# Attention projections for two batches at once, with buffers, banks and weight replacement dealt over pairs of slots

## What is computed

```
q, k, v = x @ Wq.T, x @ Wk.T, x @ Wv.T          # 16 heads: 128 plain + 64 rotary features, v 128
q_rope, k_rope = rotate(q_rope), rotate(k_rope)  # y1 = x1*c - x2*s, y2 = x1*s + x2*c
scores = q_nope @ k_nope / sqrt(128) + q_rope @ k_rope / sqrt(64)
out = softmax(scores) @ v
x   = x + out @ Wo.T
```

## Time and profile before

| | us |
|---|---|
| Time, median of 3 runs | 671.25 (671.13 to 673.66) |
| Profiled execution | 672.77 |
| Its span in the trace | 671.0 |
| PE busy | 657.5 (98%) |
| PEld busy | 633.7 (94%) |
| DVE busy | 439.2 (65%) |
| ACT busy | 410.7 (61%) |
| POOL busy | 246.4 (37%) |

### The profile page before, as it was taken

How to read it: one execution, slowest core, us unless ns; L and a number is a source line. 1 busy time by engine, 2 the same in 40 slices (tenths; PEclk the granted TensorE clock), 3 DMA queues, 4 the chain that set the end, 5 groups by cost and what they waited for, 6 DMA issues and landing times. The chain is left out here.

```text
span 671.0 us, 15275 instructions
## 1 busy us (share of the span) xinstructions
PE 657.5 (98%) x5297; PEld 633.7 (94%) x5297; DVE 439.2 (65%) x968; ACT 410.7 (61%) x1085; POOL 246.4 (37%) x279
## 2 busy tenths in 40 slices
PE   8999999999999999999999999999999999999995
PEld 8989999999999999999999899999997799999995
DVE  5665557557666656765666576556559986556877
ACT  4566677666775666866667864333689964333553
POOL 2741862134363033533328554212361462222011
PEclk9999999999999999999999999999999999999998
DMA  7074665336444435634354404100156200000000
GB/s 254 28 201 160 209 172 149 110 107 184 148 138 122 133 98 176 180 112 139 95 166 146 111 1 151 32 0 0 40 192 254 79 1 1 1 1 0 1 33 31
DMA packets 38173, 69.74 MB, mean 104 GB/s; under 512 B 3441, under 2 KB 22641, under 8 KB 37873
## 3 DMA queue, kind: packets, MB, share of 16 engines
q1 hardware_dynamic: 37696, 68.38, 33.4%
q10 hardware_dynamic: 432, 0.79, 0.4%
HBM read 52.18 MB, written 16.97 MB: 103 GB/s over the span
## 5 line engine op out<-in xcount | busy, mean ns | idle before, releaser
L312 PE MATMUL PJ<-xTh,WBh 128*128 128x256 f32 x364 | 106.7, 293 | 0.0
L314 PE MATMUL PJ<-xTh,WBl 128*128 128x256 f32 x364 | 103.0, 283 | 0.0
L313 PE MATMUL PJ<-xTl,WBh 128*128 128x256 f32 x364 | 102.8, 282 | 0.0
L830 POOL TENSOR_TENSOR stage<-stage 128x256 f32<-128x256 f32 x32 | 24.5, 765 | 165.6 <-DVE stage L697 165.6
L590 ACT ACTIVATE probs<-probs,rinv 128x256 f32<-128x256 f32 x128 | 58.4, 508 | 26.7 <-DVE rinv L713 26.7
L1208 PE MATMUL UG<-xTh,WBh 128*128 (+1 forms) x256 | 73.6, 288 | 0.3 <-PEq L54 0.3
L1211 PE MATMUL UG<-xTh,WBl 128*128 (+1 forms) x256 | 72.4, 283 | 0.0
L1209 PE MATMUL UG<-xTl,WBh 128*128 (+1 forms) x256 | 72.4, 283 | 0.0
L1280 ACT ACTIVATE ga<-UG 128x256 f32<-128x256 f32 x64 | 24.5, 383 | 75.1 <-PE UG L1211 75.1
L312 PEld LDWEIGHTS PJ<-xTh,WBh 128*128 128x128 f32 x364 | 69.6, 191 | 0.6 <-issue 0.2
L313 PEld LDWEIGHTS PJ<-xTl,WBh 128*128 128x128 f32 x364 | 69.6, 191 | 0.0
(11 more groups left out here) (320 smaller groups left out, 2389.5 us busy)
## 6 DMA issues: line engine op xcount, KB each, us to landing
K<-scr_k SPq DMA_DIRECT2D x60, 256.0 KB, 4.4
raw<-in_w_att SPq DMA_DIRECT2D x37, 256.0 KB, 4.7
Q<-scr_q SPq DMA_DIRECT2D x15, 512.0 KB, 7.6
stage<-scr_m SPq DMA_DIRECT2D x6, 768.0 KB, 4.1
scr_q<-rot_h SPq DMA_DIRECT2D x30, 128.0 KB
scr_q<-rot_l SPq DMA_DIRECT2D x30, 128.0 KB
scr_k<-rot_h SPq DMA_DIRECT2D x30, 128.0 KB
scr_k<-rot_l SPq DMA_DIRECT2D x30, 128.0 KB
```

The source lines that it names most:

```text
L312: pe.matmul(out, ah, bh, start=(i == 0), stop=False)
L313: pe.matmul(out, ah, bl, start=False, stop=False)
L314: last = pe.matmul(out, al, bh, start=False, stop=(i == n - 1))
L830: pool.tensor_tensor(y[:, 0:S], c[:, 0:S], sn[:, S:2 * S], ALU.subtract).then_inc(rope_sum, 1)
```

## The change

Queries, keys and rotary parts are projected for a pair of batches at once: one product streams 512 columns (two batches of 256 tokens) against one weight tile, where before two products streamed 256 each. The pair holds for slots 2 to 15. For that:

- slots come in pairs, an **even** slot k and the **odd** slot behind it. In an even slot TensorE projects four pieces of queries and keys in steps 0 and 1, and in steps 2 and 3 the rotary parts of the next pair in four halves (`rope_half`). In an odd slot it projects eight pieces, two in each step: two of values of its own batch, four of queries and keys, two of values. The output projection moves to step 2 (`OUT_STEP`), the addition to the residual to step 3 (`ACC_STEP`).
- the two halves of a rotary part lie in two neighbouring banks, 512 columns each: part 0 (queries) in PJ0 and PJ1, part 1 (keys) in PJ1 and PJ2. VectorE takes from such a pair of banks first one batch, then the other (`rope_part`), with two multiplications for each as before.
- `QKh[:, 0]` and `QKl[:, 0]` hold heads 0 and 1 of both batches, `[:, 1]` heads 2 and 3, where before the index was the parity of the slot.
- the rotary work of a pair is spread over both its slots on ScalarE and GpSimd; `rot_h` and `rot_l` are used twice for each pair. SyncE spills 12 times 128 KB before the first fill of a pair, and 4 times behind it.
- weights are replaced over the slots with k % 4 of 1, 2 and 3, one or two at a time, and their loads are issued over four slots.

```diff
+        def pieces(k, j):
+            if k == 15 or k % 2 == 0 and j > (2 if k == 14 else 1):
+                return []
+            return [2 * j, 2 * j + 1]
+        def has_rope(k):
+            return k % 2 == 0 and k < 14
...
-                if k < 14:
-                    spill(s + 2, k + 2, 0)
-                    spill(s + 2, k + 2, 1)
+                if has_rope(k):
+                    t, n = s + 2, 2 * (s + 2)
+                    spill(t, k + 2, 0, n, 0)
+                    spill(t + 1, k + 3, 0, n + 1, 1)
+                    spill(t, k + 2, 1, n + 2, 0)
+                    fill(t, k + 2)
+                    spill(t + 1, k + 3, 1, n + 3, 1)
+                elif k < 14:
                     fill(s + 2, k + 2)
...
+            def project_two(out, at, col, b):
+                w, toks = slice(col * P, (col + 1) * P), slice(b * S, (b + 2) * S)
+                return three(out[:, :], [(WBh[:, at + t, w], WBl[:, at + t, w]) for t in range(KT)],
+                             [(xTh[:, t, toks], xTl[:, t, toks]) for t in range(KT)])
+            def rope_half(s, k, p, half):
+                b = (k + 2) % 4
+                if p == 0 and half:
+                    if k == 0:
+                        pe.wait_ge(x_split, B)
                     if b == 0:
+                        pe.wait_ge(w_split, GP * group_of(s + 2) + 2)
+                    pe.wait_ge(part_split, 6 * s + 8)
+                elif p == 0:
+                    pe.wait_ge(part_split, 6 * s + 10)
+                elif not half:
+                    pe.wait_ge(rope_prod, 2 * s + 6)
+                last = project_two(PJ[ROPE_BANK[p] + half], 0, 2 * p + half, b)
+                if not half:
+                    last.then_inc(rope_ready, 1)
...
@@ TensorE's emit
                     scores(s, k, j)
+                    if has_rope(k) and j >= 2:
+                        rope_half(s, k, j - 2, 1)
+                    for i in pieces(k, j)[:1]:
+                        piece(s, k, i)
                     if k > 0 or j >= 1:
                         turn_probs(u - 1, (j - 1) % 4, first=(k == 0 and j == 1))
+                    if has_rope(k) and j >= 2:
+                        rope_half(s, k, j - 2, 0)
+                    for i in pieces(k, j)[1:]:
+                        piece(s, k, i)
+                    if j == OUT_STEP and k > 0:
                         output(s - 1, k - 1, first=(k == 1))
...
@@ ScalarE's part
+            def rope_part(t, k, i):
+                act.wait_ge(rope_sum, 2 * (2 * t + i) + 2)
+                rot_free(act, t, k, i)
...
@@ VectorE's emit
+                    if k % 2 and k < 14 and j == 0:
+                        rope_part(s + 1, 3)
...
                     if j in EARLY_MAX:
                         row_max(u + 1, j + 1)
-                    if j == ROPE_STEP and k < 14:
-                        part(s + 2, k + 2, 1)
+                    if has_rope(k) and j >= 2:
+                        rope_part(s + 2, 2 * (j - 2))
+                    for i in pieces(k, j)[1:]:
+                        part(s, k, i)
                     if (k > 0 or j >= 2) and not (k == 14 and j == 1):
                         oT(u - 2, k if j >= 2 else k - 1, (j - 2) % 4)
+                    if has_rope(k) and j == 2:
+                        rope_part(s + 2, 1)
```

More of the change, by code:

```diff
@@ L119, in attention @@
         rope_lo = sem("rope_lo")
-        spill_q = sem("spill_q")
-        spill_k = sem("spill_k")
+        spill_done = [sem(f"spill_done{i}") for i in range(2)]
         stack_q = [sem(f"stack_q{i}") for i in range(2)]
@@ L208, in _, with spill @@
         def _(sp):
-            def spill(s, k, i):
-                scr, spilled = ((scr_q, spill_q), (scr_k, spill_k))[i]
-                for part, src, done in ((0, rot_h, rope_hi), (1, rot_l, rope_lo)):
-                    sp.wait_ge(done, 2 * s + i + 1)
+            def spill(s, k, i, m, at):
+                scr = (scr_q, scr_k)[i]
+                for part, src, ready in ((0, rot_h, rope_hi), (1, rot_l, rope_lo)):
+                    sp.wait_ge(ready, m + 1)
                     for half in range(2):
-                        sp.dma_start(scr[k % 2, 2 * part + half].rearrange("p j n -> j p n"),
-                                     src[:, i, half, :].bitcast(F32)).then_inc(spilled, 16)
+                        sp.dma_start(scr[k % 4, 2 * part + half].rearrange("p j n -> j p n"),
+                                     src[:, at, half, :].bitcast(F32)).then_inc(spill_done[k % 2], 16)
             def fill(s, k):
@@ L359, in piece @@
-            def piece(s, k, p):
-                b = k % 4
-                out = bank_of(k, p)
-                bank_free(s, k, p)
-                if b == 0 and p % 2 == 0:
-                    pe.wait_ge(w_split, GP * (s // 4 if isinstance(s, int) else group[0]) + 2 + p)
-                if p < 6:
-                    last = project(out, p, slice(b * S, b * S + S))
-                else:
-                    rows = slice(b * S + (p - 6) * P, b * S + (p - 5) * P)
-                    last = three(out[:, :], [(xTh[:, t, rows], xTl[:, t, rows]) for t in range(KT)],
-                                 [(WBh[:, 6 + t, :], WBl[:, 6 + t, :]) for t in range(KT)])
+                    pe.wait_ge(x_split, slot + 1)
@@ new lines, in first_rope, with first_piece @@
+                    if slot == 0:
+                        pe.wait_ge(w_split, 2)
+                if slot:
+                    pe.wait_ge(rope_prod, p + 1)
+                project(first_rope_bank(p), p, slice(slot * S, slot * S + S)).then_inc(rope_ready, 1)
+            def first_piece(p):
+                if p == 6:
+                    pe.wait_ge(part_split, 1)
+                if p == 7:
+                    pe.wait_ge(part_split, 2)
+                if p % 2 == 0:
+                    pe.wait_ge(w_split, 2 + p)
+                if p < 6:
+                    last = project(first_bank(p), p, slice(0, S))
+                else:
+                    last = values_in(first_bank(p), p - 6)
+                last.then_inc(piece_ready, 1)
@@ new lines, in values_in @@
+            def values_in(out, tile):
+                rows = slice(tile * P, (tile + 1) * P)
+                return three(out[:, :], [(xTh[:, t, rows], xTl[:, t, rows]) for t in range(KT)],
+                             [(WBh[:, 6 + t, :], WBl[:, 6 + t, :]) for t in range(KT)])
+            def project_two(out, at, col, b):
+                w, toks = slice(col * P, (col + 1) * P), slice(b * S, (b + 2) * S)
+                return three(out[:, :], [(WBh[:, at + t, w], WBl[:, at + t, w]) for t in range(KT)],
+                             [(xTh[:, t, toks], xTl[:, t, toks]) for t in range(KT)])
@@ L373, in piece, with query, key @@
                 last.then_inc(piece_ready, 1)
+            def query(part, k, j, rows):
+                if k < 2:
+                    return part[:, k, j, rows]
+                return part[:, j // 2, 2 * (j % 2), (k % 2) * S + rows.start:(k % 2) * S + rows.stop]
+            def key(part, k, j):
+                if k < 2:
+                    return part[:, k, j, S:2 * S]
+                return part[:, j // 2, 2 * (j % 2) + 1, (k % 2) * S:(k % 2 + 1) * S]
             def scores(s, k, j):
@@ L629, in emit @@
                     exps(u, j)
-                    if k < 15:
-                        for p in ORDER[j][0]:
-                            part(s + 1, k + 1, p)
-                    if j == ROPE_STEP + 1 and k < 14:
-                        part(s + 2, k + 2, 0)
+                    for i in pieces(k, j)[:1]:
+                        part(s, k, i)
+                    if has_rope(k) and j == 3:
+                        rope_part(s + 2, k, 0)
                     if k > 0 or j >= 1:
```

413 lines of the change are left out of this document (239 added, 174 removed).

## The result

The changed kernel takes 710.7 us (median of 6 runs, 706.8 to 712.3); the one before took 673.2 beside it. The ratio is 1.056, with a 95% interval of 1.054 to 1.057: 37.5 us slower, where I had forecast 21. Its profiled execution took 711.85 us, with a span of 710.0.

A forecast was written before the change was run, and what follows sets the result against it. PE, busy 98%, was taken to bound the kernel through its order of work. Terms -4.3 + 16.8 + 3.6 + 4.4 - 1.0 + 1.7 = +21.2 us on the median 671.25 gave 692.5, forecast as 692; range 683 to 702.

The forecast's parts named there:

- The projection, -4.3: Slots 2 to 15: 504 fewer products save some 8 ns each, 0.61 us per pair, 4.3 us in all.
- rival d: Weight loads set PE's pace, so a 512-column product costs no more than a 256-column one: 636 us, chance 0.01.
- The wait for rope_prod, +16.8: Step 3 of even slots 0 to 12: PE waits 2.4 us for VectorE's query products, 7 times, 16.8 us.
- Nothing covers it: PE's queue is in order, with values and next scores behind the step 3 wait, so all 16.8 us count.
- The fills, +3.6: Even slot starts: 12 spills before the keys' fill, not 8, cost 0.6 us in each of six steady pairs, bounds 0 and 12.
- I take 0.6, near the short end: PE's wait for the keys' fill per pair, chosen between no stall and 2 us.
- T + 29.6 to T + 31.0: Keys' landing, counted from T, the end of head 3's scores on PE; PE wants them at T + 29.65.
- (c): Rival: DMA decides, the 12 spills go at the 8's pace, odd slots also begin late: 706 us, chance 0.13.
- (b): Rival: VectorE's query products finish before head 3's row maximum, so PE gains: 667 us, chance 0.09.
- The first pair, +4.4 - 1.0: Late first spills and slot 2's keys cost 4.4 us; 1.0 off for slot 1's earlier pause falling into moved time.
- Cost at nothing: weight replacement: Weight replacement, moved to other steps, adds at most one 0.63 us ScalarE copy per step, beside PE's work: 0.
- The end, +1.7: Slot 15: the output projection moves from step 3 to step 2, costing 1.7 us, bounds 0 and 3.

The follow-up runs named there:

- e12 in halves: e12 with the projection of two batches as twice 256 columns in place of once 512: 680.1 us, ratio 1.010.
- e18: e12 with the scratch laid out head by head, so spills have 128 rows outermost, and fills cut into 32-partition pieces: 668.7 us, ratio 0.995.
- e1: Changed kernel with VectorE's products of the query part ahead of the row maximum of head 3: 709.2 us, ratio 1.052.
- e19: Changed kernel with only the scratch laid out head by head (faster spills) and fills cut into 32-partition pieces: 702.3 us, ratio 1.045.
- e17: Changed kernel with VectorE's products ahead of the row maximum and the head-by-head scratch layout for faster spills: 680.6 us, ratio 1.012.
- e2: Changed kernel with 17 unused products of 256 columns on TensorE ahead of its step 3 wait: 713.5 us, ratio 1.060.
- e3: Changed kernel with both VectorE products directly behind the row maximum of head 3 and OTl only behind them: 711.2 us, ratio 1.057.
- e15: e12 with ScalarE's rounding that waits for the first spills one step later, in slot 1 only: 677.9 us, ratio 1.008.
- e11: e1 plus ScalarE's first two roundings earlier, e4's and e5b's edits, and one remainder of slot 14 ahead of a row maximum: 685.0 us, ratio 1.020.
- e12: e11 with GpSimd rotating ahead of its split of weight tile 4 in every second pair: 677.1 us, ratio 1.005.
- e5b: Changed kernel with slot 15's output projection put back into step 3 and the accumulation behind everything: 707.5 us, ratio 1.051.
- e14: e12 with the 2 MB of loads ahead of the first spills issued from ScalarE's queue: 678.2 us, ratio 1.010.
- e4: Changed kernel with slot 0's three weight loads issued behind its spills and GpSimd's twelve adds moved into slot 1: 706.4 us, ratio 1.051.
- e8: Changed kernel with the even slot's keys spilled ahead of the odd slot's queries: 733.2 us, ratio 1.092.
- e13: Changed kernel with two more 128 KB writes per pair on the spills' queue, to a buffer nobody reads: 727.2 us, ratio 1.080.

## Why the prediction was right and where it was wrong

Right were the direction, the place, cause and size of the main wait, the small gain of the projection and the times of SyncE's queue; wrong was the total, 710.7 against a range that ended at 702. In the profiled run the next layer starts 17.5 us later than forecast: 6.5 of them arise in slots 14 and 15 (the term for the end, +1.7, was mis-sized), 6.0 in the five steady pairs (half clock behind the wait had no term, and the fills' was too small), 4.1 in the pair from slot 2 (weight replacement, put at nothing, and a wait for keys) and 0.9 before slot 2.

- **The projection, -4.3.** -3.0 by e12 in halves. That the weight loads set the pace (rival d) is refuted, since twice 256 columns cost almost what once 512 does. Rival (d) quoted the Trainium skill (Perfetto Trace Analysis, Identifying the Most-Contended Engine), which takes the busy share of LDWEIGHTS, beside the share of peak FLOPs, for the measure of TensorE. That share is 94% in the kernel before, 87% in the changed one and 91% in e18, the fastest; it falls with the 504 loads that are gone as well as with PE's waits, so alone it ranks e18 below the kernel before, which is slower.
- **The wait for rope_prod, +16.8.** It is 15.1 on PE, in all seven places. What failed is the step "Nothing covers it", though not as a rival had it: the wait ran beside another loop of nearly the same length, so that taking it away alone gave 2 us (e1), partly because the half clock moved behind the waits for keys, and 22, with the half clock, once that loop was short (e19 to e17).
- **The half clock, not in the sum.** After a pause of 2.2 us I let PE go on at 0.23 us for each product of 512 columns. It went on at 0.43 in five of seven places, 1.3 to 1.5 us each. In the kernel as it is, taking this away alone gave nothing that shows (e2, e3). Beside fast spills it is part of the 22 us.
- **The fills, +3.6.** The issues came at the forecast times, and the waits for keys add up to 2.4 us. But "I take 0.6, near the short end" is the step that failed for the steady pairs. The pairs without any slow stretch in e2 and e3 still take 50.6 to 51.2 us, 3.5 over before in the mean, where I had 2.4; the fill had to be taken at some 1.7 us, near the 2 us of its bound. The keys are there some 31 to 31.7 us after T, at or behind the late end of my T + 29.6 to T + 31.0. The trace hid this, because the slow stretches moved PE's demand back by as much.
- **The rivals.** (c), "DMA decides", was the nearest at 706 and had 0.13. It was right that the 12 spills decide; its mechanism, an odd slot that begins late, did not occur. (b) is e1's edit. It was priced with the fills on time, and they were not.
- **The first pair, +4.4 - 1.0.** The stretch to slot 2 grew by 6.3 with the first wait in it, forecast 5.4. The parts were others: 3.7 us in slot 1 (forecast 1.7) and some 2 at half clock, and no wait for slot 2's keys (forecast 2.7). e15 shows these two to be one: what the one place does not wait, the other does.
- **Cost at nothing: weight replacement.** It failed once, in slot 2. I looked at ScalarE's copies and not at GpSimd, where the split of the second rotary weight now stood behind 9 us of adds: 3.2 us. In the kernels without the step 3 wait, GpSimd's split of tile 4 ahead of the rotation costs another 8 us (e11 to e12; 10 by the ratios).
- **The end, +1.7.** It is 7.3 from slot 15 on, and slot 14 is 0.9 over its forecast. I moved the output projection and left out what moved with it: the accumulation, now in step 3 with the reciprocal of the last head behind it on VectorE, and the half clock behind the pauses that this makes. Putting slot 15 back takes 5.1 off the slot (e5b).

So, by runs that differ in one edit, and by their ratios: 7 us for the slow spills (e19), 22 for the wait of step 3 with its slow stretches (e19 to e17), and 8 left in e17 against the kernel before. By the starts in e17's trace, whose profiled run is 6.9 us longer than that of the kernel before, they are -3.6 up to slot 2 (1.6 of it before slot 0, whose start lies between 22.2 and 24.6 from run to run), +4.4 in the pair from slot 2 (GpSimd's adds, 3.1, and half clock behind that wait), -1.7 in the five steady pairs and +7.8 in slots 14 and 15. Of the 22 us some 15 are the wait itself (7 times 2.1) and the rest half clock; this is an estimate from the pairs of e19. The split by runs holds for this order of edits only, since each alone gives less.

The placing in e14 could not tell whether the first spills' place in the queue matters beside their pace, and it stays open; with fast spills that wait is gone (e19).

## What to carry to other kernels

When a new wait stands beside a transfer that lands "just in time", price the longer of the two loops and not their sum, and then ask which one remains when either is removed: here one cure alone gave 1.5 to 2 us (e1), the other 7 to 8 (e19) and both together 30. Look at what stands behind a wait that has moved, too: PE's half clock moved with it. Before reordering transfers, look at the share of DMA engines in a window where they run alone; a share near a quarter with a full queue asks for another layout, not another order. For every operation that is moved, follow what each in-order engine now has ahead of it, GpSimd's slow background work and the softmax's short steps above all.

## What the hardware showed that I had not expected

- In step 3 of the even slots, the first one left out, a pause of PE of 2.18 to 2.24 us was followed by half clock (0.52 in the window shown) in 5 of 6 cases in the changed kernel, in 5 of 6 in e4, 6 of 6 in e5b, 3 of 6 in e19 and none of 6 in e8 and e13 each; pauses of 1.85 to 1.91 us in none of 6 in e3. With PE fed through the same time the clock held in all seven (e2).
- e1, e8 and e13 had their half clock behind the waits for keys instead (5, 6 and 5 of 6). There too the length does not decide: in e2 a wait of 1.9 us was followed by it and one of 2.0 was not, in e1 one of 2.0 was and one of 2.3 was not. No run here shows what else does.
- At the low clock a product of 512 columns started every 0.43 us in place of 0.23, for some 2.5 us.
- 128 KB written in rows of 1 KB with 4 heads as the outer dimension moved at 93 GB/s; the same bytes with 128 rows outermost at 273 GB/s.
